# Attention's last 40 steps taken together with the first projection of the MLP, and the prologue in another order (one core of a Trainium2)

## The reference

```python
ada = silu(c) @ Wada.T + bada
shift_msa, scale_msa, gate_msa, shift_mlp, scale_mlp, gate_mlp = split(ada, 6)
h = rmsnorm(x, g1, D) * (1 + scale_msa) + shift_msa
q, k, v = (h @ Wqkv.T + bqkv) in 16 heads of 32
q = rmsnorm(q, gq, 32) * 32 ** -0.5;  k = rmsnorm(k, gk, 32)
o = softmax(q @ k.T) @ v
x = x + gate_msa * (o @ Wproj.T + bproj)
h = rmsnorm(x, g2, D) * (1 + scale_mlp) + shift_mlp
x = x + gate_mlp * (gelu(h @ Wfc1.T + bfc1) @ Wfc2.T + bfc2)
```

## Time and profile before

| | before |
|---|---|
| time, median of 3 runs | 1812.02 us (1808.69 to 1813.46) |
| the profiled execution, its time / its span | 1810.62 / 1808.8 us |
| PE busy | 1727.9 us, 96%, 8376 matmuls |
| DVE busy | 1085.6 us, 60% |
| ACT busy | 919.6 us, 51% |
| POOL busy | 372.5 us, 21% |

### The profile page before, as it was taken

The page is one execution under the profiler, slowest core; times in us unless marked ns, Lnnn a source line. Parts: engine busy times, 40 slices in busy tenths (PEclk is TensorE's granted clock), DMA queues, the critical chain, the costliest instruction groups (busy, mean ns, idle before and its releaser), DMA issues.

```text
span 1808.8 us, 23247 instructions
## 1 busy us (share of the span) xinstructions
PE 1727.9 (96%) x8376; PEld 1154.5 (64%) x8376; DVE 1085.6 (60%) x1325; ACT 919.6 (51%) x1136; POOL 372.5 (21%) x305
## 2 busy tenths in 40 slices
PE   6998999999999999999889999999999999999998
PEld 3554555555555555554224787878788887878786
DVE  6678888898898898878788545142332324142301
ACT  4476666777777777778787432222221212221221
POOL 3001111100001000000140233333332333333332
PEclk8999999999999999999999899999999999999999
DMA  5754545555555555555765201010020202010000
GB/s 195 214 144 132 135 123 139 132 147 135 154 135 134 146 130 156 127 135 153 174 144 196 74 18 58 25 52 24 12 70 6 64 17 64 17 52 23 17 18 24
DMA packets 122242, 176.92 MB, mean 98 GB/s; under 512 B 29568, under 2 KB 43904, under 8 KB 121136
## 3 DMA queue, kind: packets, MB, share of 16 engines
q1 hardware_dynamic: 115952, 156.41, 32.3%
q10 hardware_dynamic: 5408, 16.81, 2.5%
q0 software_dynamic: 800, 2.62, 0.5%
HBM read 124.87 MB, written 50.92 MB: 97 GB/s over the span
## 4 chain that ended last, share of the span: by engine, by line
PE 44%; issue 29%; DVE 11%; POOL 9%; ACT 4%; DMA 2%; SPq 0%; POOLq 0%; ACTq 0%; DVEq 0%
PE scores L513 9%; PE pv L530 8%; PE gemm L588 7%; DVE sums L791 5%; PE scores L1303 5%; POOL act_parts L1235 5%; PE gemm L601 4%; ACT probs L704 3%; PE pv L1320 3%; PE gemm L1320 2%; PE aux L554 2%; POOL y L1233 2%; PE aux L547 1%; DVE raw L816 1%; DVE raw L862 1%
## 5 line engine op out<-in xcount | busy, mean ns | idle before, releaser
L704 ACT ACTIVATE probs<-scores,shift 128x1024 f32<-128x1024 f32 x512 | 548.7, 1113 | 195.4 <-PE scores L513 178.7
L791 DVE TENSOR_TENSOR sums<-sums,probs 128x2048 f32<-128x2048 f32 x192 | 453.8, 2363 | 32.7 <-ACT probs L704 28.0
L513 PE MATMUL scores<-q_stack,k_stack 128*128 128x512 f32 x1024 | 358.8, 435 | 6.3 <-ACT probs L704 6.1
L1303 PE MATMUL scores<-w_hi,act_parts 128*128 128x512 f32 x1024 | 318.7, 392 | 0.0
L513 PEld LDWEIGHTS scores<-q_stack,k_stack 128*128 128x128 f32 x1024 | 173.8, 189 | 202.3 <-issue 105.5
L1235 POOL TENSOR_TENSOR act_parts<-act_full,act_parts 128x512 fp32r<-128x512 f32 x128 | 172.5, 1348 | 514.2 <-ACT act_parts L1166 513.6
L530 PE MATMUL pv<-probs,v 128*32 128x512 f32 x2048 | 253.1, 603 | 0.4 <-ACT probs L704 0.4
L1303 PEld LDWEIGHTS scores<-w_hi,act_parts 128*128 128x128 f32 x1024 | 191.4, 189 | 38.8
L1303 PE MATMUL scores<-w_lo,act_parts 128*128 128x512 f32 x512 | 199.9, 391 | 0.0
L1373 DVE TENSOR_TENSOR y_next<-pv,p_bias 128x512 f32<-128x512 f32 x28 | 19.3, 691 | 299.7 <-PE pv L1275 299.7
L1166 ACT ACTIVATE act_parts<-act_full 128x512 fp32r<-128x512 f32 x128 | 80.9, 632 | 224.5 <-PE scores L1303 223.5
(11 more groups left out here) (167 smaller groups left out, 1944.1 us busy)
## 6 DMA issues: line engine op xcount, KB each, us to landing
k_stack<-parts_scratch SPq DMA_DIRECT2D x128, 256.0 KB, 5.0
q_stack<-parts_scratch SPq DMA_DIRECT2D x128, 256.0 KB, 5.1
parts_scratch<-parts SPq DMA_DIRECT2D x62, 512.0 KB, 2.9
inverse<-inverse_scratch SPq DMA_DIRECT2D x128, 64.0 KB, 2.1
heads_out<-o_out SPq DMA_DIRECT2D x32, 256.0 KB, 5.2
out<-result SPq DMA_DIRECT2D x32, 256.0 KB, 2.0
heads<-heads_out SPq DMA_DIRECT2D x28, 256.0 KB, 3.6
x_tile<-in_x SPq DMA_DIRECT2D x28, 256.0 KB, 2.8
```

Source lines behind the costliest of these rows:

```text
L513: mm = nc.tensor.matmul(scores[p][:, i, :], k_stack[s][:, h, j * P:(j + 1) * P], q_stack[half][:, h, :], start=True, stop=True)
L704: nc.scalar.activation(probs[L % RING][:, 2 * p:2 * p + 2, :], scores[p][:], ACT.Exp, bias=small["shift"][:]).then_inc(exp_done, 1)
L791: nc.vector.tensor_tensor(sums[:], a[:], probs[l % RING][:], ALU.add).then_inc(added, 1)
L1303: mm = nc.tensor.matmul(acc[t], act_parts[m % 2][:, b, t * P:(t + 1) * P], w2[a][:, m, :], start=(m == 0 and i == 0), stop=(m == NM - 1 an ...
```

## The change

Three things. **In the last 48 steps**, `PAIRED` becomes `AFTER`: the weighings stay in pairs to the end of attention. From unit `LEAN` = 26 (step 208) on, VectorE makes six adds instead of seven, and `row_sums` adds the eighth key tile with four more ones-matmuls on `probs` (`adds_until` counts the adds; ScalarE may overwrite that tile only after them). **Chunk 0's projection** is made in the steps 222 to 249, 7 steps to a tile, one or two matmuls in each (`step` in place of `first_projection`), all four tiles in one bank (`up[0]`, `gemm`), so a tile waits for the one before to be moved (`proj_moved`). Gate and residual, square, clamp and norm follow in the steps 229 to 253; heads and x are loaded and split earlier; the normed tiles and `z_full` get buffers for four tiles each (`y_norm_first`, `z_full_first`). `last` then turns the four tiles at once; ScalarE modulates tiles 1 and 3 and VectorE 0 and 2, whole, where each had half of every tile; `move_rows` for the last unit and four of the eight MLP weight loads come behind the z copies, and `low1(1)` behind the z tiles. **In the prologue** the order of the first products is v0, k0, q0, v1 to v4, k, q (9 before step 0, where there were 10; v5 moves into the steps), the norm and turn steps are shifted, both row moves precede the first weight split on ScalarE, and the ada weight loads are issued at its start, right behind those of `wstage`.

```diff
-START, AFTER_LAST = -25, 2
-PLAN = placed(-18, 0, [v_of(0, 1), v_of(1, 1), v_of(2, 1), k_of(0, 0, 1), q_of(0, 0, 1), v_of(3, 1), v_of(4, 1), v_of(5, 1),
-                       k_of(0, 1, 1), q_of(0, 1, 1)])
+START, AFTER_LAST = -27, 2
+PLAN = placed(-18, 0, [v_of(0, 1), k_of(0, 0, 1), q_of(0, 0, 1), v_of(1, 1), v_of(2, 1), v_of(3, 1), v_of(4, 1), k_of(0, 1, 1), q_of(0, 1, 1)])
...
-SPLIT_W = {"act": {-23: 0, -20: 1, -17: 2}, "dve": {-20: 0, -19: 1, -16: 2}}
-ROW_MM, ROW_MOVED, MOD_TURN, MOD_MADE, GAINS = {-25: 0, -24: 1}, {-24: 0, -22: 1}, -23, -20, -18
-ADA_LOAD, ADA_BIAS, ADA_MM, ADA_MADE, ADA_STORED = -14, -9, -8, -5, 2
+SPLIT_W = {"act": {-24: 0, -20: 1, -18: 2}, "dve": {-22: 0, -20: 1, -19: 2}}
+ROW_MM, ROW_MOVED, MOD_TURN, MOD_MADE, GAINS = {-27: 0, -26: 1}, {-26: 0, -25: 1}, -25, -23, -18
+ADA_BIAS, ADA_MM, ADA_MADE, ADA_STORED = -9, -10, -5, 2
...
+LEAN = -(-max(FILL) // NT)
+
+
+def adds_until(l):
+
+    hh, j = l // NT, l % NT
+    return ADDS * min(hh, LEAN) + (ADDS - 1) * max(0, hh - LEAN) + (min(j, ADDS - 1) if hh >= LEAN else j)
+
+
...
-PAIRED = max(FILL)
-HEADS_LOAD, BIAS_LOAD, X_LOAD = {TAIL + 2 + 3 * t: t for t in range(CT)}, TAIL + 14, {TAIL + 17 + 3 * t: t for t in range(CT)}
-HEADS_HIGH, HEADS_LOW, X_BIASED = ({TAIL + after + 2 * t: t for t in range(CT)} for after in (18, 19, 34))
+PAIRED = AFTER
+PROJ_STEPS = 7
+PROJECT = {TAIL + 9 + PROJ_STEPS * t + i: (t, i) for t in range(CT) for i in range(PROJ_STEPS)}
+HEADS_LOAD, BIAS_LOAD, X_LOAD = {TAIL + t: t for t in range(CT)}, TAIL + 5, {TAIL + 6 + t: t for t in range(CT)}
+HEADS_HIGH, HEADS_LOW = ({TAIL + after + 3 * t: t for t in range(CT)} for after in (6, 7))
+X_BIASED = {TAIL + 11 + 3 * t: t for t in range(CT)}
+PROJ_OUT, PROJ_SQUARE, PROJ_CLAMP, PROJ_NORM = ({TAIL + 9 + PROJ_STEPS * (t + 1) + after: t for t in range(CT)} for after in range(4))
...
-            pe.wait_ge(added, ADDS * (hh + 1))
+            pe.wait_ge(added, adds_until(NT * hh + NT - 1))
             aux_free()
...
+            if hh >= LEAN:
+
+                l = NT * hh + NT - 1
+                pe.wait_ge(exp_done, 2 * l + 2)
+                for h in range(HG):
+                    mm = nc.tensor.matmul(aux[h * DH:(h + 1) * DH, :], small["ones"][:], probs[l % RING][:, h, :], start=False, stop=True)
...
             high1(0)
             high1(1)
...
-            move_rows()
-            square(0)
-            square(1)
-            high1(2)
+            load_w2(0)
+            load_w1(1)
+            load_w2(1)
             act.wait_ge(pv_mm, AFTER)
...
+            first_z(1)
             turn_tile(0, 0)
...
             turn_tile(0, 1)
-            act.preload_act_table(ACT.Gelu_apprx_tanh)
+            first_z(3)
             turn_tile(0, 2)
             turn_tile(0, 3)
+            move_rows()
+            act.preload_act_table(ACT.Gelu_apprx_tanh)
+            high1(2)
             high2(0)
             high2(1)
...
+            if lo == 0:
+                pe.wait_ge(heads_lo, t + 1)
+                if t == 0:
+                    pe.wait_ge(wp_low, KT)
+                    pe.wait_ge(raw_done, len(UNIT))
+                else:
+                    pe.wait_ge(proj_moved, t)
+            k, a, b = terms[lo]
+            mm = nc.tensor.matmul(up[0], z[b][:, k, r], wp[a][:, k, :], start=(lo == 0), stop=(lo == len(terms) - 1))
```

More of the change, by code:

```diff
@@ L119 @@
 HOUT += [step + 1 for step in TURN[NT:]]
[L120 removed]
+SPLIT = [-21, -20, -19, -18, -15, -14, -13, -12] + [step + 1 for step in HOUT[NT:]]
 STAT_AT, NORM_AT, TURN_AT, SPLIT_AT = ({step: n for n, step in enumerate(table)} for table in (STAT, NORM, TURN, SPLIT))
@@ L715, in scalar @@
         setup["scalar_first"](act)
+        for i in range(NA_LATER):
+            cols = slice((NA_NOW + i) * CH, (NA_NOW + i + 1) * CH)
+            act.dma_start(ada_w[i], dram["wadaT"][:, cols].rearrange("(k p) n -> p k n", p=P)).then_inc(ada_w_in[i], 16)
         for L in range(START, AFTER):
@@ L779, in add @@
             j, hh = l % NT, l // NT
-            if j == 0:
+            if j == 0 or hh >= LEAN and j == NT - 1:
                 return
@@ L935, in build_mlp @@
     gated = result[0][:]
+    first = [y[:, t, :] for t in range(CT)]
     scores, pv = psum["scores"], psum["pv"]
@@ L1345, in chunk @@
             down(c, NM - 1, first_two + last_two)
-        return last
+        return step, last
     def vector(dve):
```

170 lines of the change are left out of this document (80 added, 90 removed).

## The result

The changed kernel takes 1847.78 us (1845.79 to 1849.41, 4 runs) where before takes 1811.03 (4 runs): a ratio of 1.0201, 95% interval 1.0189 to 1.0213, or +36.8 us. The forecast was +14, range 1804 to 1840. The sign was right, the size not. From here on, "the tail" is the time from the first exponential of step 208 to the end of the last one of step 255, a cycle is two steps, "the turn" is the passage from attention to the MLP, and a "+" before a time in the turn counts from the end of the last exponential.

What follows compares the result with a forecast made beforehand. No engine was taken to be full in the last 48 attention steps; a chain in TensorE's program order sets the pace. Tail +27.0, turn -10.0, prologue -3.6 and clock +1 put 1810.6 at 1825 us, range 1804 to 1840.

Steps and rivals of the forecast that it cites:

- paired weighing: Last 48 steps: two weighings in each odd step lengthen the cycle from 4.69 to 5.55 us, 23 times, +19.8.
- Rival 1: Last 48 steps: pairing costs nothing because VectorE's adds carry the steps; 19.8 go off, 1805 us; chance 0.20.
- the 11.9: Last 48 steps: 11.9 us of VectorE stalls in the kernel before, taken to vanish altogether with six adds fewer.
- Eighth tile: Row sums of the last 48 steps: added ones-matmuls on TensorE make them cost 9.6 us, where 5.0 was.
- Projection matmuls: Chunk 0's projection inside the steps: ten matmuls of 0.23 fall behind the scores of an odd step, +2.3 us.
- rival 4: Tail: TensorE works less densely and gets the half clock for long stretches, about 1870 us; chance 0.05.
- (a): Step 219: ScalarE's copy of the heads waits for four loads, holding later exponentials, +3.7 us (0 to 6).
- (b): Steps 229, 236, 243: the next tile's first projection matmul waits for VectorE to empty the one bank, +8.5 us (0 to 11).
- The turn: Attention to MLP: first MLP matmul at +8.9 for +22.8, gain shrunk by the late last output to 10.0 us (6 to 16).
- The gather I put at 2: Last unit's chain in the turn: the gather of the stored row sums was taken at 2 us.
- The prologue: Before the first exponential: earlier row moves and new order give -6.3, v5 in the steps +2.7; net -3.6 us (-8 to +5).
- Rival 3: Prologue: ada loads share the DMA engines evenly with wstage, weights up to 13.9 us later, 9 taken; 1834 us; chance 0.08.

Runs made afterwards that it cites:

- b_lean: The kernel before with only the eighth key tile's row sum moved to TensorE in the last 48 steps; 1804.91 us, ratio 0.9959.
- a_nolean: The changed kernel with seven adds per unit on VectorE to the end and no ones-matmuls for the eighth key tile; 1848.01 us.
- a_gap: The changed kernel with a matmul-free step between projected tiles and VectorE's move one step earlier, ahead of that step's add; 1834.64 us.
- a_rows_loads: The changed kernel with the last row sum and its copy first, and four MLP weight loads issued later, at hidden tile 2 of chunk 0; 1853.05 us.
- a_rows_first: The changed kernel with the last unit's row sum ahead of the four turns and its copy ahead of the z copies; 1849.02 us.
- b_prologue: The kernel before with the whole new prologue, early ada loads included, and the old tail; 1823.41 us, ratio 1.0055.
- b_pro_ada18: The kernel before with the new prologue, but the four ada weight loads at step -18; 1815.36 us, ratio 1.0025.

## Why the forecast was right in sign and wrong in size

The tail was forecast to cost, and it did; the measured time lies above the whole range. Three terms of the sum account for it: the ada loads and the new order of the prologue, 12.6 us; the half clock behind the stalls of the tail, 9.2; the turn, 2.9, in which the gather of the row sums is the step that failed.

- **What bounds the tail, and paired weighing.** Right: 5.54 for 5.55, 7.26 for 7.3. Rival 1 (pairs cost nothing) fell. Its reason had a part in it: taken from before alone, pairs cost 12 and not 20, since one of the two large stalls behind VectorE goes with them. The sum had that, as the 11.9 set to nothing.
- **Eighth tile.** Right: b_lean 7.4 faster. Beside pairs it is worth nothing (a_nolean), so its gain and the vanished stalls were one and the same.
- **Projection matmuls.** 0.23 us in a cycle (5.77 for 5.54), as forecast.
- **Half clock for long stretches (rival 4).** It did not come: from 874 to 886, paired weighings without a stall, the granted clock is 1.00. Its 1870 was also wrong by its own terms: 1.7 us in each of 23 cycles are 39, so at most 1864.
- **(a) The heads, forecast 3.7.** The wait was 5.7, a cycle of 10.42 for 5.54, +4.9, and the next one, which begins at half clock, 7.99 for 5.54, +2.5: 7.3.
- **(b) The bank, forecast 8.5.** 228 to 230 takes 11.88, 236 to 238 7.79, 242 to 244 11.73: 14.1 in all over the 5.77 of a cycle with projection and no wait, and a_gap took 13.5 out of the tail. The waits were in the right places and, at 3.29, 2.17 and 3.29, of the right length; their price was mis-sized, for I took "+1" for the clock where three of the four stalls drew stretches at half clock of their own. Together (a) and (b) are 9.2 us more than forecast, and 156.0 + 9.2 = 165.2 for the 164.8 measured. The row for it stood in the prediction (matmuls at half clock); I had priced it once, not once for each stall that I forecast myself.
- **The turn, forecast -10.0, measured -7.1.** First MLP matmul right. "The gather I put at 2" is the step that failed: it took 7.4, and the output came at +24.4 for +22, the store ahead of the gather giving back 3.1 (1.7 for 4.8). The 2 had no row behind it, and before's own trace had 7.2 for this gather: it was issued at 987.83 and landed at 995.1, with the engines at 426 GB/s from 988 to 995. And what bounds the turn is not `low2(0)`, as I said, but the first projection of chunk 1, behind the same chain and the same traffic. That the traffic holds the store of the reciprocals and the spread is shown: a_rows_loads and a_rows_first differ in the four loads alone. For the gather it is read from three traces, 7.4 and 7.2 us with the engines full, 1.5 in a_rows_first at a share of 0.44; no run changes only that.
- **The prologue, forecast -3.6, measured +9.0** (10.3 between the means of the kernels with either prologue at step 64, 10.0 by b_prologue's ratio). This is the largest miss, 12.6 us of the 23 by which the span misses. The step: "in my sum they cost nothing, since they stand behind wstage on its own queue". They stood behind it on the queue, and ScalarE stood behind them. The rule of the skill that I cited is about the transfers, and these did as it says: `wstage` landed at 18.60, 21.98 and 25.37, in before at 18.26, 22.31 and 25.81. The Trainium skill, "DMA: Bandwidth & Descriptors", Issuing engines are not separate DMA queues, calls the time on the sequencer to start a DMA usually small beside the DMA itself. Here the issues took 6.60, 3.10, 3.43 and 2.72 us, so the measurement decides. Rival 3 added 9 for a late `wstage`; the early loads cost 4.4 to 5.3, and by another mechanism. The second failed step is "the modulation is made near 17.8": it waits for `bada_cols`, which lands between 21.0 and 21.6 in every kernel here, before included, so it comes at 21.09 even with the ada loads out of the way. With it go "v(0) at 24.6, k(0) at 30.0, q(0) at 33.2", which were 28.23, 35.66 and 40.21; the 2.0 and 1.4 us by which k(0) and q(0) fell further behind are waits for an h tile and for VectorE's `v`, by the brackets of their rows. And v5 in the first steps, forecast 2.7, would have 3.9 at step 64 if all of that is its.

## What to carry to other kernels

A DMA that is issued early can hold the engine that issues it: put bulk loads behind the work that the engine owes to others, or on an engine that owes nothing. Price a wait on TensorE's path with the half clock behind it: here two waits of 3.3 us cost 6 each, one of 2.2 only itself. Take the time of a small transfer from the trace at the place where it stands, with the traffic that it meets. When a wait is taken away and the time stays, look for the next holder and ask what they all stand behind; and test the parts of a bundle singly: here one part was worth -7 us and the bundle +37.

## What the runs showed of the hardware that I had not expected

- The issue of a 1 MB load on ScalarE took 6.60 us with three such loads ahead on its queue, then 3.10, 3.43, 2.72; in b_pro_ada18, at 29 us, the same issues took 0.37, 0.53, 0.53 and 0.85. In a_rows_loads SyncE stood 8.34 us in the issue of a 256 KB load at 1046.21, with four 1 MB weight loads under way on ScalarE's queue.
- TensorE's granted clock was 0.50 at 899 to 903 us behind 5.68 us of idleness and at 931 to 936 behind 3.29 us; the pair of weighings took 3.64 us instead of 1.92. Behind 2.17 us of idleness it stayed at 1.00.
- The gather of the row sums, 8 KB, landed after 7.4 us with the DMA engines 96% busy at 377 GB/s; the median of all 32 such gathers is 1.7.
